# Flamingo gated cross-attention on one core: the negated maxima turned by one product and spread over eight query rows by DVE, instead of eight products and one row copied by ACT

## What is computed

```python
q = layernorm(x) @ qw.T + qb          # (16, 56, 128)
k = ctx @ kw.T + kb                   # (16, 1500, 128)
v = ctx @ vw.T + vb
scores = einsum('bhqd,bhkd->bhqk', split(q) * 8 ** -0.5, split(k))
scores = where(mask[:, None] == 0, -1e9, scores)
probs = softmax(scores, axis=-1)      # exp(scores - max over the keys) / its sum
out = einsum('bhqk,bhkd->bhqd', probs, split(v))
x = x + tanh(g_xattn) * (merge(out) @ ow.T + ob)
x = x + tanh(g_ffn) * moe(layernorm(x))
```

## Time and profile before

| | |
|---|---|
| time, median of 3 runs | 600.38 us (599.91 to 600.98) |
| the profiled execution, its own time | 604.03 us |
| its span, first to last instruction | 602.2 us |
| PE busy, share of the span | 514.7 us, 85% |
| DVE busy | 403.9 us, 67% |
| ACT busy | 329.6 us, 55% |
| POOL busy | 153.6 us, 25% |
| all DMAs, mean over the span | 124 GB/s |
| L338, eight products a unit, 128 in all | 210 to 215 ns each |
| L437, the copy of the row, 16 in all | 909 ns each |

### The profile page before, as it was taken

How to read it: one execution, slowest core, us unless ns; L and a number is a source line. 1 busy time by engine, 2 the same in 40 slices (tenths; PEclk the granted TensorE clock), 3 DMA queues, 4 the chain that set the end, 5 groups by cost and what they waited for, 6 DMA issues and landing times.

```text
span 602.2 us, 15674 instructions
## 1 busy us (share of the span) xinstructions
PE 514.7 (85%) x6779; PEld 354.6 (59%) x6779; DVE 403.9 (67%) x748; ACT 329.6 (55%) x408; POOL 153.6 (25%) x134
## 2 busy tenths in 40 slices
PE   0610879999999999999999999999999559999993
PEld 0200437667676666666667676676676455777773
DVE  6701578677686776876768767677674745787756
ACT  0200155666656656566565665656656507877782
POOL 8320532504325053250532505235000000000000
PEclk9855699999999999999999999999999866999997
DMA  9499678768677686766957669664400400120001
GB/s 212 103 266 196 133 171 184 169 155 167 155 167 163 155 173 152 172 151 147 190 147 178 144 148 189 152 130 105 91 2 3 120 22 2 36 72 1 2 2 30
DMA packets 40125, 74.62 MB, mean 124 GB/s; under 512 B 3935, under 2 KB 26592, under 8 KB 40057
## 3 DMA queue, kind: packets, MB, share of 16 engines
q1 hardware_dynamic: 38456, 71.37, 51.3%
q10 hardware_dynamic: 1600, 2.26, 2.2%
HBM read 26.09 MB, written 0.46 MB: 44 GB/s over the span
## 4 chain that ended last, share of the span: by engine, by line
PE 71%; DVE 15%; issue 5%; SPq 4%; DMA 3%; ACT 2%; POOL 0%; POOLq 0%; DVEq 0%; ACTq 0%
PE ring L330 14%; PE pv L368 12%; PE st L351 10%; DVE max_part L493 8%; PE ring L313 8%; PE ring L276 8%; PE st L653 7%; PE ring L692 5%; PE pv L374 3%; DMA keys<-k_lo 2%; DVE recip L522 2%; PE pv L692 1%; PE ring L861 1%; PE ring L338 1%; SPq L748 1%
## 5 line engine op out<-in xcount | busy, mean ns | idle before, releaser
L493 DVE TENSOR_REDUCE max_part<-ring 112x1 f32<-112x512 f32 (+1 forms) x384 | 245.3, 673 | 113.5 <-PE ring L330 113.5
L448 ACT ACTIVATE probs<-st 128x896 f32<-128x896 f32 x192 | 175.6, 915 | 104.1 <-PE st L351 101.2
L330 PE MATMUL ring<-keys,qrs 121*112 121x512 f16 (+1 forms) x384 | 141.9, 394 | 30.3 <-DMA keys<-k_lo 22.2
L351 PEld LDWEIGHTS st<-qrs,keys 121*128 121x128 f16 (+1 forms) x1536 | 89.2, 101 | 42.1 <-ACT qrs L437 13.5
L553 POOL TENSOR_TENSOR k_hi<-k_raw,zero 128x512 f16<-128x512 f32 (+1 forms) x48 | 49.5, 1032 | 251.7 <-ACT k_raw L416 224.9
L351 PE MATMUL st<-qrs,keys 121*128 121x112 f16 (+1 forms) x1536 | 108.5, 214 | 2.0 <-ACT qrs L437 2.0
L368 PE MATMUL pv<-probs,v_ext 128*32 128x168 f32 (+1 forms) x1536 | 94.5, 318 | 0.3 <-DVE sums L513 0.2
L330 PEld LDWEIGHTS ring<-keys,qrs 121*112 121x112 f16 x384 | 46.7, 131 | 55.5 <-DVE max_part L493 25.9
L416 ACT ACTIVATE k_raw<-ring,biases 128x512 f32<-128x512 f32 (+1 forms) x48 | 32.5, 677 | 66.6 <-PE ring L276 64.9
L276 PE MATMUL ring<-ctxT,w_qkv 128*128 128x512 f32 (+1 forms) x96 | 57.4, 682 | 11.0 <-DMA ctxT<-in_ctx 7.8
L368 PEld LDWEIGHTS pv<-probs,v_ext 128*32 128x32 f32 (+1 forms) x1536 | 30.3, 108 | 46.3 <-issue 33.8
(11 more groups left out here) (105 smaller groups left out, 385.0 us busy)
## 6 DMA issues: line engine op xcount, KB each, us to landing
ctxT<-in_ctx SPq DMA_DIRECT2D x16, 750.0 KB, 4.3
keys<-mask_add SPq DMA_DIRECT2D x32, 375.0 KB
keys<-k_hi SPq DMA_DIRECT2D x32, 375.0 KB, 6.0
keys<-k_lo SPq DMA_DIRECT2D x32, 375.0 KB, 7.0
keys<-mask_add SPq DMA_DIRECT2D x32, 281.2 KB
mask_raw<-in_mask SPq DMA_DIRECT2D x16, 375.0 KB, 3.9
up_w<-in_up_w SPq DMA_DIRECT2D x9, 256.0 KB, 2.8
down_w<-in_down_w SPq DMA_DIRECT2D x9, 256.0 KB, 3.2
```

Of the source, the lines that this page charges most:

```text
L330: nc.tensor.matmul(ring[0:QW, m % 2, 0:width(c)], qrs[0:ROWS, w, p, :, :].rearrange("r h q -> r (h q)"), keys[0:ROWS, w, p, chunk(c)], sta ...
L351: mm = nc.tensor.matmul(st[0:m, j % 2, p // 4, QW * (p % 4):QW * (p % 4 + 1)], keys[0:ROWS, u, p, j * P:j * P + m], qrs[0:ROWS, u, p, :, : ...
L448: nc.scalar.activation(probs[0:m, j % 3, :].rearrange("p (h c) -> p h c", h=2), st[0:m, j % 2, :, 0:HQ // 2], ACT.Exp).then_inc(s["exps_do ...
L493: nc.vector.tensor_reduce(max_part[:, p, c:c + 1], ring[0:QW, m % 2, 0:width(c)], AX.X, ALU.max).then_inc(s["max_read"], 1)
```

## The change

The keys get eight rows of ones (rows 96 to 103), one per pair, and the stack grows from 121 to 128 rows. `neg_max` is turned by one product with eight output rows, one per pair. DVE then writes all eight query rows at once: for row r and pair p it takes row r of the product times `pair_row[r, p]`, which is one where r is p and zero elsewhere, so that the sum over the eight rows of ones gives each pair its own maximum. ACT's copy is gone. The new operation stands in DVE's order right behind the merge of the maxima, ahead of the next unit's mask.

```diff
-NR = S + 1
+NR = S + PAIRS
...
+    pair_row = np.zeros((P, PAIRS), np.float32)
+    pair_row[ONEROW:ONEROW + PAIRS] = np.eye(PAIRS)
...
-        ones_row = sb("ones_row", [1, NK], F16)
+        ones_row = sb("ones_row", [PAIRS, NK], F16)
...
-                    for r0, r1 in ((0, QSPLIT), (QSPLIT + 1, NR)):
+                    for r0, r1 in ((0, QSPLIT), (QSPLIT + PAIRS, NR)):
...
-            for p in range(PAIRS):
-                mm = nc.tensor.matmul(ring[ONEROW:ONEROW + 1, p // 4, QW * (p % 4):QW * (p % 4 + 1)],
-                                      neg_max[:, p:p + 1], ident_h[:, :], start=True, stop=True)
-            mm.then_inc(s["max_turned"], 1)
+            nc.tensor.matmul(ring[ONEROW:ONEROW + PAIRS, 0, 0:QW], neg_max[:, :], ident_h[:, :],
+                             start=True, stop=True).then_inc(s["max_turned"], 1)
...
-        def act_max_row(act, b):
-
-            k, u, t = b
-            act.wait_ge(s["max_turned"], k + 2)
-            nc.scalar.activation(qrs[ONEROW:ONEROW + 1, buf(b, 1), :, :, :]
-                                 .rearrange("r (x p) h q -> r x (p h q)", x=2),
-                                 ring[ONEROW:ONEROW + 1, 0:2, 0:4 * QW], ACT.Copy).then_inc(s["max_copied"], 1)
-
...
-                if j == TURN_STEP and has(k, 1):
-                    act_max_row(act, b)
...
+        def dve_max_rows(dve, b):
+
+            k, u, t = b
+            rows = slice(ONEROW, ONEROW + PAIRS)
+            dve.wait_ge(s["max_turned"], k + 2)
+            nc.vector.tensor_tensor(qrs[rows, buf(b, 1), :, :, :].rearrange("r p h q -> r p (h q)"),
+                                    ring[rows, 0:1, 0:QW].to_broadcast([PAIRS, PAIRS, QW]),
+                                    pair_row[rows, :].unsqueeze(2).to_broadcast([PAIRS, PAIRS, QW]),
+                                    ALU.mult).then_inc(s["max_copied"], 1)
...
                     dve_merge_max(dve, b)
+                    dve_max_rows(dve, b)
...
-            sp.dma_start(keys[ONEROW:ONEROW + 1, :, :, :].rearrange("r u p k -> r (u p) k"),
-                         ones_row[:, :].unsqueeze(1).to_broadcast([1, NB * PAIRS, NK])).then_inc(s["ones_placed"], 16)
+            sp.dma_start(keys[ONEROW:ONEROW + PAIRS, :, :, :].rearrange("r u p k -> r (u p) k"),
+                         ones_row[:, :].unsqueeze(1).to_broadcast([PAIRS, NB * PAIRS, NK])).then_inc(s["ones_placed"], 16)
```

More of the change, by code:

```diff
@@ L60, in constants @@
     spread = (row[:, None, None] == den[None]).astype(np.float32)
-    skip = np.insert(np.eye(S, dtype=np.float32), QSPLIT, 0.0, axis=0)
+    skip = np.insert(np.eye(S, dtype=np.float32), [QSPLIT] * PAIRS, 0.0, axis=0)
     mask_row = np.zeros((P, S), np.float32)
@@ L66, in constants @@
     onehot[0:NR] = np.tile(skip.astype(np.float16) * np.float16(BIG), (1, B))
+    pair_row = np.zeros((P, PAIRS), np.float32)
+    pair_row[ONEROW:ONEROW + PAIRS] = np.eye(PAIRS)
     rank = np.tile(np.arange(E, 0, -1, dtype=np.float32), (P, TT))
     return {
-        "c_f32": np.concatenate([np.eye(P, dtype=np.float32), spread.reshape(P, 2 * P), own], axis=1),
+        "c_f32": np.concatenate([np.eye(P, dtype=np.float32), spread.reshape(P, 2 * P), own, pair_row], axis=1),
         "c_rows": mask_row,
@@ L84, in sem @@
             return ctx.enter_context(nc.semaphore(name))
-        c_f32 = sb("c_f32", [P, P + 2 * P + HG])
+        c_f32 = sb("c_f32", [P, P + 2 * P + HG + PAIRS])
         ident = c_f32[:, 0:P]
@@ L90, in flamingo_kernel @@
         own = c_f32[:, 3 * P:3 * P + HG]
+        pair_row = c_f32[:, 3 * P + HG:3 * P + HG + PAIRS]
         c_rows = sb("c_rows", [P, S])
@@ L1025 @@
         arrays["mask"][:, MROW * h:MROW * h + QSPLIT] = mask[:, 0:QSPLIT, h]
-        arrays["mask"][:, MROW * h + QSPLIT + 1:MROW * h + NR] = mask[:, QSPLIT:S, h]
+        arrays["mask"][:, MROW * h + QSPLIT + PAIRS:MROW * h + NR] = mask[:, QSPLIT:S, h]
     m = np.arange(D)
```

## The result

The changed kernel takes 620.16 us (median of 4 runs, 619.29 to 621.52), the kernel before 600.68 (4 runs): slower by 19.5 us, a ratio of 1.0325 with a 95% interval of 1.0297 to 1.0354. The forecast was 617.8, its range 602 to 622. The profiled execution of the changed kernel took 621.52 us.

The account below looks back on a forecast made before the run. PE was taken to bound the kernel, with 71% of the chain. Fourteen units at 1.27 us more (17.8), less 0.4 for two turns, gave +17.4 us and 617.8 us; range 602 to 622.

Parts of the forecast that it names:

- The gain of the turn: At the turn between units, L351 can start at 234.17 instead of 234.36: 0.19 us won each turn.
- the prediction's sum: Unit with keys: POOL's and DVE's holds delay the fourth score, 1.27 us longer; fourteen units and two gaining turns: +17.4 us.
- seven products at 0.35: On PE at the turn, one product replaces eight; the seven dropped cost 0.35 us.
- The exclusion: DVE's SBUF-to-SBUF operations with one tensor source and POOL's operations exclude each other; whichever comes first holds the other to its end.
- The mis-sized term: Each unit with mask and keys becomes 1.27 us longer, fourteen units giving 17.8 us.
- two maxima, 0.60 and 0.61 us: On DVE after `any_row` in a unit: two maxima end at 237.96 and 238.57, releasing the third and fourth plain scores.
- POOL's lead: In a unit, `k_hi` starts at 234.85, ahead of `mask_add` at 234.87, so POOL goes first by 0.02 us.
- the case that I gave 0.55: In the units POOL's `k_hi` goes first and holds `mask_add`; kernel at 617.8 us, chance 0.55.
- `k_lo` stretched by some 0.3: Expected sign in the changed profile: POOL's `k_lo` in the units takes some 0.3 us longer.
- Rival 1: In the units DVE's `mask_add` goes ahead of `k_hi`: 0.26 us a unit longer, +3.2 us, 603.6; chance 0.24.
- Rival 2: In the units the exclusion does not matter; the whole 3.0 us gain stays, 597.4; chance 0.11.
- rival 3: Later mask pushes DMAs or second chunk's split, 0.3 us a unit, or rows of ones delay start, 4: some 622; chance 0.10.

Follow-up runs that it names:

- experiment 1: Changed kernel with the mask's three DVE operations put back in front of the writing of the query rows: 600.83 us against 601.86 for the kernel before.
- experiment 4: Changed kernel with the new DVE operation writing only four pairs, the other four pairs' maxima left out: 601.48 us, ratio 0.999 to the kernel before.
- experiment 7: Changed kernel with the mask ahead of the write and PE's turning product ahead of the last products with the values: 596.43 us against 601.44.
- experiment 2: Changed kernel plus one wait: POOL's first split of a unit waits until DVE has done `any_row`: 599.40 us, ratio to before 0.9974.
- experiment 8: Kernel before with POOL's first MEMSET written over half as many elements of twice the size: 596.92 us against 601.44.
- experiment 5: Changed kernel with the new DVE operation writing seven pairs instead of eight, the eighth pair's maximum left out: 621.33 us.
- experiment 6: Changed kernel with the new DVE operation writing six pairs instead of eight, two pairs' maxima left out: 605.83 us, ratio 1.0061.
- experiment 3: Kernel before plus one wait: DVE starts the next unit's mask only when ACT has copied the row of maxima: 609.37 us, ratio 1.0120.

## Why the prediction was right

**Where the time lies.** As predicted, in the units with keys and mask: from the first L340 to the last the changed kernel takes 477.84 − 81.95 = 395.89 us, the one before 459.11 − 82.07 = 377.04 from L338 to L338. That is 18.9 us of the 19.5; the start and the experts differ by less than the runs do. Inside the unit it lies ahead of the fourth plain score: from the products with the values behind that score to the next turn the changed kernel takes 20.37 us (246.82 to 267.19), the one before 20.38 (237.70 to 258.08).

**The gain of the turn.** Predicted 0.19 us, with the write at 1.09 us and DVE 0.04 us behind the product. Measured 0.16 in experiment 1, 0.18 by the unit: the write takes 1.096 us and starts 0.06 behind. The estimate by the Trainium skill, VectorE: DVE Perf Modes, section on the TRN2 errata (1.058 us), is 38 ns short, and it was the one figure that put DVE first in the prediction's sum. What experiments 4 and 7 add is that the turn gives 0.47 to 0.48 when the write no longer ends last; the prediction priced seven products at 0.35 and left out the weights that PE can then load ahead. The kernel before does not quite hide its copy: it starts L351 1.09 us behind L276 at the turn and 0.96 behind it inside the unit (235.82 to 236.78), so 0.13 us of the turn was still a wait for ACT's copy. The turns without a product of the keys take the same 1.58 us (435.17 to 436.75). In experiment 4 the weights of L352 are loaded from 233.07 and its first product starts at 233.23; in the kernel before, both start at 234.36.

**The exclusion.** It was read from three rows of the start, and experiments 1, 2 and 8 show it in three ways: with the mask moved ahead, with POOL held back, and with the POOL operation shortened, each DVE operation returns to its own time. Experiments 5 and 6 show who wins: the one that begins first, by 0.06 or 0.07 us either way, and by 0.01 in experiment 3. The prediction's wording, "from SBUF to SBUF with one tensor source", takes in too much: `mask_abs` is such an operation and is not part of it. The steps from the earlier trace rows held to 0.01 us in the changed kernel: `mask_add` ends 0.40 after `k_hi`, `k_lo` 1.01 after `mask_add`, `any_row` 0.05 after `k_lo`. The Trainium skill, SBUF — State Buffer, section "SBUF: two separate sides", describes just this as an exclusive lock on a shared pair of ports that the first takes for the whole instruction; the runs agree in who waits and for how long, and do not show the ports.

**The mis-sized term.** The unit was priced at 1.27 us more and came out at 1.38. That is 1.4 us over units 1 to 13. Unit 0 came out at 0.94, 0.33 less than priced, and unit 14 is 0.04 us shorter where 0.19 was priced, though its turn gained 0.16; where the difference lies in it is not shown. Together the units took 1.25 us more than the sum, of the 2.1 us between the forecast change, 17.4, and the measured 19.5; the rest is within what the runs vary by. That the forecast of the profiled execution, 621.4, met 621.52 is in part luck: outside the units the profiled execution of before was 1.4 us longer than that of the changed kernel. The step inside the unit is "two maxima, 0.60 and 0.61 us": the prediction let the first maximum start before `any_row` ends, and it starts 0.04 behind (245.09 to 245.13). The same overlap is missing between L501 and `mask_abs` (241.88 to 241.90, where the prediction had 0.09 of overlap); that, with the write's later start and its 1.10 us, made POOL's lead 0.16 us instead of 0.02. So the case that I gave 0.55 was in fact clear, but by an effect that I did not know of: that my own 0.02 us lay on the right side was luck. Experiment 3, built on the kernel before, has the overlap behind `any_row` (236.42 to 236.34). Being held is not what takes it away: in experiment 2 `any_row` takes 0.24 us and the overlap is missing all the same (235.89 to 235.93). In experiment 7 it is missing between `any_row` and L501 (230.59 to 230.63). What the three places share is L501, which works on rows 96 to 103, where the others start at row 0: each is L501 itself, or the first operation behind it that reads SBUF or that reads PSUM. That fits the profiles, but no run tests it. The sign "`k_lo` stretched by some 0.3" was at odds with the sum, which has `k_lo` at 1.34 us instead of 1.16; 1.34 is what it took.

**The rivals.** Rival 1, priced at 0.26 us a unit, was real, but not for this kernel; experiments 3, 4 and 6 are its cases, at 0.58, 0.06 and 0.29. Rival 2 is out by the rows of the changed kernel, where `mask_add` and `any_row` are held. Of rival 3, the later mask pushed nothing else onto the path, by the 20.37 us above. The rows of ones fill the pause of the DMA engines that the prediction named: idle at 20 to 22 us before, they are busy there now, as this window of the changed kernel shows (share in the last column but one). DVE and POOL are not later for it at 27 us (`mask_add` at 26.59, before 26.60), and the first L340 is at 81.95, where L338 was at 82.07. But with one profile of each and a start that varies by more, a price of a few us between 30 and 82 us is not excluded.

```profile
20.00:22.00 2.00, 2.00 (x6) 0.67 (x4) 2.00 (x2) 0.00 (x0) 0.00 (x0) 1.00 0.99 118
```

## What to carry to other kernels

Before an operation is put in front of others on an engine, look at what the other engines do at the time to which those others slip; in these runs `mask_add`, `any_row` and L720, DVE operations of the kind TENSOR_SCALAR from SBUF to SBUF, and POOL's operations held each other to the end. The sign is an instruction that takes longer than usual (`mask_add` 2.4 times, L720 some 25 times) and ends right behind one of the other engine, a held DVE instruction 0.03 to 0.4 us behind it. Reductions and operations that read PSUM were not held, so what stands in front of what can be chosen. The place in the order was worth more here than the work: the same product and the same write cost 19.5 us in one order, nothing that the whole time can show in a second, and gained 5 us in a third, where the product was earlier too. A long operation of an engine that "has nothing to do" is worth a look too: the MEMSET at the start cost 4.2 us on an engine that it shares no data with.

## What the runs showed that I had not expected

- The order of two engines is settled on differences of 0.01 to 0.06 us, and stays the same through units 1 to 13 of a run: `any_row` took 1.14 us in all of them with seven pairs, and 1.03 with six. In unit 0 it can differ: with seven pairs nothing was held there.
- The overlap of two DVE instructions, 0.08 to 0.09 us, is missing at two places of the changed kernel, held or not, and present at one of them in a kernel built on the one before. Both are the first of their kind behind the write to rows 96 to 103; whether that is the cause is open.
- POOL's MEMSET over 64 x 14336 elements of 2 bytes takes 12.04 us, and over 64 x 7168 of 4 bytes, the same bytes, 6.07.
